# Node numbers and the weighing's exponentials in one PSUM bank for VectorE; each exponential taken twice

## The chip, the cores and the metric
One core of a Trainium2 chip. The metric is the time of one launch in microseconds (us) on the device, as the median of several runs. Engines: PE is TensorE (PEld its weight load), DVE is VectorE, ACT is ScalarE, POOL is GpSimd, and SP only issues transfers.

## What is computed
The network takes 6250 node rows of 256 numbers and 200000 edges sorted by destination. `x` is normalised, a graph transformer of two attention layers and a linear attention ("mix") over all nodes are added to it, and then a mixture of experts with a graph router. The change lies in the two attention layers:

```python
def gt_layer(edge_index, embeds, qT, kT, vT, ln_s, ln_b):      # D = 128, HEAD = 8 heads of 16
    rows, cols = (edge_index[0], edge_index[1])
    q = (embeds[rows] @ qT).reshape(-1, HEAD, hd)
    k = (embeds[cols] @ kT).reshape(-1, HEAD, hd)
    v = (embeds[cols] @ vT).reshape(-1, HEAD, hd)
    att = jnp.clip(jnp.einsum('ehd,ehd->eh', q, k), -10.0, 10.0)
    expAtt = jnp.exp(att)
    attNorm = jax.ops.segment_sum(expAtt, rows, num_segments=n)[rows]
    att = expAtt / (attNorm + 1e-08)
    res = (att[..., None] * v).reshape(-1, d)
    agg = jax.ops.segment_sum(res, rows, num_segments=n)
    # then: add embeds, layer norm
```

## The kernel before
The kernel sorts the edges by the tile of 125 nodes that their `rows` end lies in (50 tiles), so that each tile of 128 edges belongs to one node tile. `attend` then works through 1668 edge tiles in 417 groups of four (GROUP = 4). It is called twice, as att1 (with `Keys` beside it, which prepares the linear attention) and att2 (with `Mix` beside it, which finishes it). Nothing else uses the changed lines.

A group passes these stations. GpSimd issues four indirect gathers (L700), each of 128 rows of 256 numbers (keys and values) from HBM to `kv_e`, a ring of four groups (SLOTS = 4). SP loads the node numbers of the edges as rows (`local`, L681). VectorE compares them with a pointer scalar `lane_no` into `hot_t` (near_hot, L811, one SBUF tensor of 512 bf16 values). TensorE multiplies `hot_t` with the node tile's queries into PSUM `ps_q` (fetch_q, L761). VectorE forms the products of `ps_q` with the keys (dots, L798), sums them by head (sum_dots, L817) and clips the sums (clip, L830). ScalarE takes the exponential into the last 8 columns of `vals` (exps, L784). VectorE multiplies the values with these exponentials (weigh, L822: both inputs in SBUF, the exponentials repeated 16 times). It also builds the one-hot matrix `hot` by comparing `node_no`, 500 node numbers held in SBUF, with the edges' own (one_hot, L804: both inputs in SBUF). TensorE adds up `hot` times `vals` into PSUM `ps_sum` (add_up, L773), and VectorE adds that to `acc` (add_sums, L838, twice per group).

The order on each engine is written out by hand: `edge_steps` unrolls all steps, and in step n each part handles group n plus its lag. VectorE's list is

```python
            edge_steps(dve, total, [(0, dots), (2, near_hot), (0, sum_dots), (-1, weigh), (0, clip), (1, one_hot),
                                    (-2, add_sums)], lambda n: side.vector(dve, n), side.last)
```

so that it weighs group n-1 between the head sums and the clip of group n. `side` is `Keys` or `Mix`, whose instructions stand behind each step's on each engine; a node tile of theirs is spread over steps 8 apart. A gather of group k waits until group k-4 has been weighed (`used=m["weighted"]` in `gather_rows`). `vals`, `clipped`, `hot_t`, `ps_q` and `ps_sum` are double buffers; `prod` is single. In att2 all eight PSUM banks are held: two `ps_q`, two `ps_sum` and Mix's `ps_t`, `ps_q`, `ps_o`, `ps_h`.

Of the kernel before, what the change touches and what calls it, by code (L numbers as in the profile page):

```python
# [7 lines left out]
ALU = mybir.AluOpType  # L8
# [8 lines left out]
LANES = 128  # L17
# [692 lines left out]
def attend(nc, c, name, g, qs, kv, acc, beside):  # L710

    with ExitStack() as st:
# [3 lines left out]
        def psum(n):  # L716
# [9 lines left out]
        vals = sb("vals", [LANES, 2, GROUP, SUMS])  # L726
        tile_of = sb("tile_of", [1, g.pairs], I32)
        ps_q, ps_sum = psum("ps_q"), psum("ps_sum")
        m = sem_set(nc, st, name, ["tiles_in", "one_hots", "near_hots", "q_ready", "prods",
                                   "dots", "clips", "exps", "weighted", "summed", "added"])  # L730
        m["gathered"] = c.gathered[name]
        m["local_in"] = st.enter_context(semaphores(nc, [f"{name}_local_in{j}" for j in range(SLOTS)]))
        total = g.edge_tiles // GROUP
# [15 lines left out]
        @block.tensor  # L749
        def _(pe):  # L750
            pe.wait_ge(m["tiles_in"], 16)
            numbers = TileNumbers(nc, pe, tile_of, g)

            def fetch_q(k, r, j):

                pe.wait_ge(m["near_hots"], k + 1)
                wait(pe, m["prods"], k - 1)
                for p in range(per):
                    t = numbers.of(k * per + p)
                    for e in range(PAIR * p, PAIR * (p + 1)):  # L760
                        ins = pe.matmul(ps_q[j % 2][:, e * D:(e + 1) * D], hot_t[:, j % 2, e * LANES:(e + 1) * LANES],  # L761
                                        at(qs, t), start=True, stop=True)
                ins.then_inc(m["q_ready"], 1)
                numbers.load((k + 1) * per)

            def add_up(k, r, j):

                pe.wait_ge(m["weighted"], k + 1)
                pe.wait_ge(m["one_hots"], k + 1)
                wait(pe, m["added"], 2 * (k - 2) + 2)  # L770
                for p in range(GROUP // PAIR):
                    for e in range(PAIR):
                        ins = pe.matmul(ps_sum[j % 2][0:NODE_TILE, p * 256:p * 256 + SUMS],  # L773
                                        hot[:, j, PAIR * p + e, :], vals[:, j % 2, PAIR * p + e, :],
                                        start=e == 0, stop=e == PAIR - 1)
                ins.then_inc(m["summed"], 1)
            edge_steps(pe, total, [(-2, add_up), (1, fetch_q)], lambda n: side.tensor(pe, n), side.last)

        @block.scalar
        def _(act):  # L780
            def exps(k, r, j):
                act.wait_ge(m["clips"], k + 1)
                wait(act, m["summed"], k - 1)
                act.activation(vals[:, j % 2, :, D:SUMS],  # L784
                               clipped[:, j % 2, :].rearrange("p (e h) -> p e h", e=GROUP), ACT.Exp)\
                    .then_inc(m["exps"], 1)
            edge_steps(act, total, [(0, exps)], lambda n: side.scalar(act, n), side.last)

        @block.vector
        def _(dve):  # L790
            dve.wait_ge(m["tiles_in"], 16)
            numbers = TileNumbers(nc, dve, tile_of, g)

            def dots(k, r, j):
                dve.wait_ge(m["q_ready"], k + 1)
                dve.wait_ge(m["gathered"][j], (r + 1) * (16 * GROUP))
                wait(dve, m["dots"], k)
                dve.tensor_tensor(prod[:].rearrange("p (e d) -> p e d", e=GROUP),  # L798
                                  ps_q[j % 2][:, :].rearrange("p (e d) -> p e d", e=GROUP),
                                  kv_e[:, j, :, 0:D], ALU.mult).then_inc(m["prods"], 1)  # L800

            def one_hot(k, r, j):
                wait(dve, m["summed"], (k - SLOTS) + 1)
                dve.tensor_tensor(hot[:, j], c.node_no[:],  # L804
                                  own_tile(g, k), ALU.is_equal)\
                    .then_inc(m["one_hots"], 1)

            def near_hot(k, r, j):
                dve.wait_ge(m["local_in"][j], (r + 1) * 16)
                wait(dve, m["q_ready"], k - 1)  # L810
                dve.tensor_scalar(hot_t[:, j % 2, :], local[0:NODE_TILE, j], c.lane_no[0:NODE_TILE, :], None, ALU.is_equal)\  # L811
                    .then_inc(m["near_hots"], 1)

            def sum_dots(k, r, j):
                dve.wait_ge(m["prods"], k + 1)
                wait(dve, m["clips"], k - 1)
                dve.tensor_reduce(dots_sb[:, j % 2, :], prod[:].rearrange("p (h d) -> p h d", d=HEAD),  # L817
                                  AX, ALU.add).then_inc(m["dots"], 1)

            def weigh(k, r, j):  # L820
                dve.wait_ge(m["exps"], k + 1)
                dve.tensor_tensor(vals[:, j % 2, :, 0:D].rearrange("p e (h d) -> p e h d", d=HEAD),  # L822
                                  kv_e[:, j, :, D:2 * D].rearrange("p e (h d) -> p e h d", d=HEAD),
                                  vals[:, j % 2, :, D:SUMS].unsqueeze(3).broadcast_to([LANES, GROUP, HEADS, HEAD]),
                                  ALU.mult).then_inc(m["weighted"], 1)

            def clip(k, r, j):
                dve.wait_ge(m["dots"], k + 1)
                wait(dve, m["exps"], k - 1)
                dve.tensor_scalar(clipped[:, j % 2, :], dots_sb[:, j % 2, :], -10.0, 10.0, ALU.max, ALU.min)\  # L830
                    .then_inc(m["clips"], 1)

            def add_sums(k, r, j):
                dve.wait_ge(m["summed"], k + 1)
                for p in range(per):
                    a = at(acc, numbers.of(k * per + p))
                    wait(dve, m["added"], 2 * k + p)
                    dve.tensor_tensor(a, a, ps_sum[j % 2][0:NODE_TILE, p * 256:p * 256 + SUMS], ALU.add)\  # L838
                        .then_inc(m["added"], 1)
                numbers.load((k + 1) * per)  # L840
            edge_steps(dve, total, [(0, dots), (2, near_hot), (0, sum_dots), (-1, weigh), (0, clip), (1, one_hot),
                                    (-2, add_sums)], lambda n: side.vector(dve, n), side.last)


# [137 lines left out]
class Mix:  # L982

    def __init__(self, nc, c, ins, st, X, mean, rstd, mean_rstd, mix_rstd, key_values, key_sums):
# [16 lines left out]
        self.square, self.scaled = self.xr, sb("scaled", [NODE_TILE, GIN])  # L1001
        self.shift = sb("shift", [NODE_TILE, GIN])
        self.ms = sb("ms", [NODE_TILE, self.tiles])
        self.ps_t, self.ps_q, self.ps_o, self.ps_h = (psum(n) for n in ("ps_t", "ps_q", "ps_o", "ps_h"))
        self.m = sem_set(nc, st, "mix", ["w_in", "w_ready", "normed", "turned", "turned_sb", "q_ps", "q_copied",
                                         "q_min", "q_exped", "q_ready", "o_ps", "den", "inverse", "o_ready", "h_ps",
                                         "h_base", "h_out", "squared", "stepped", "shifted", "ms", "root", "roots", "scaled",
# [117 lines left out]
    def tensor(self, pe, n):  # L1125
        m, two = self.m, self.two
        t = self.tile_at(n, 3)
        if t is not None:
            pe.wait_ge(m["normed"], t + 1)
            wait(pe, m["turned_sb"], t)  # L1130
            for ch in range(KC):
                turn = pe.transpose(self.ps_t[:, ch * NODE_TILE:(ch + 1) * NODE_TILE],
                                    self.xr[:, ch * LANES:(ch + 1) * LANES], self.c.ident[0:NODE_TILE, 0:NODE_TILE])
# [1311 lines left out]
```

## Time and profile before

| | us |
|---|---|
| runs, median of 3 (lowest, highest) | 7925.82 (7924.39, 7932.85) |
| the profiled execution, its own time | 7930.16 |
| its span | 7927.9 |
| att1 (1218 to 3410 of the span) | 2192 |
| att2 (3515 to 5706) | 2191 |
| busy over the span: PE, DVE, ACT, POOL | 5293.5, 5852.9, 1022.4, 5163.2 |

Busy shares are averages over stages with different limits. What is worth reading for this change are the two attention stages. An engine's busy time counts its own instructions; the time from one gather's end to the next one's start is not in it.

### The profile page before, as it was taken

What the parts mean: (1) busy time and instruction counts of PE and PEld (TensorE: products, weight loads), DVE (VectorE), ACT (ScalarE), POOL (GpSimd) and SP (SyncE); (2) the same over time, 40 slices, a digit from 0 to 9 for tenths busy, and PEclk for the clock granted to TensorE, in tenths of its full rate; (3) what the DMA queues carried; (4) which work ended last, traced back from release to release, by engine and by line L of the source; (5) the groups of instructions that cost most, each with busy time, mean ns of one, the idle gap of its engine ahead of it and who ended that gap; (6) DMA issues with size and microseconds to landing.
All of it is one profiled execution on the core that took longest, in us unless ns stands there. A gap on an engine that the chain in (4) does not pass through costs nothing. (4 is left out here: it accounts for less than half of the span.)

```text
span 7927.9 us, 103405 instructions
## 1 busy us (share of the span) xinstructions
PE 5293.5 (67%) x27325; PEld 4204.5 (53%) x27325; DVE 5852.9 (74%) x15897; ACT 1022.4 (13%) x3273; POOL 5163.2 (65%) x5420
## 2 busy tenths in 40 slices
PE   5886855665665566556666666666559999999441
PEld 3553534555555555535555555555546666666331
DVE  7878845666666666667787878877766777777997
ACT  0000010000000000020000000000132222222230
POOL 2331306777777777737777777777617777777892
PEclk7555578778778877877887778878758888888555
DMA  1000034444444444434444444444432333332336
GB/s 31 3 3 8 3 95 125 129 128 129 128 129 128 128 129 130 128 97 126 126 127 126 125 125 126 126 125 126 125 82 52 63 62 57 62 63 55 114 96 179
DMA packets 504010, 776.97 MB, mean 98 GB/s; under 512 B 121545, under 2 KB 364222, under 8 KB 503442
## 3 DMA queue, kind: packets, MB, share of 16 engines
q0 software_dynamic: 202656, 454.22, 21.7%
q1 hardware_dynamic: 292838, 304.95, 14.7%
q10 hardware_dynamic: 7948, 11.21, 0.6%
q8 instruction: 237, 3.88, 0.2%
q14 instruction: 331, 2.71, 0.1%
HBM read 698.60 MB, written 71.36 MB: 97 GB/s over the span
## 5 line engine op out<-in xcount | busy, mean ns | idle before, releaser
L700 POOL DMA_INDIRECT att_kv_e<-kv,gnn_idx x3336 | 3366.1, 1009 | 1196.5 <-issue 1004.8
L773 PE MATMUL att_ps_sum<-att_vals,att_hot 128*125 128x136 f32 x6672 | 1345.1, 361 | 1638.6 <-DVE att_vals L822 1637.8
L773 PEld LDWEIGHTS att_ps_sum<-att_vals,att_hot 128*125 128x125 f32 x6672 | 1131.4, 246 | 1852.8 <-DVE att_vals L822 1845.7
L700 POOL DMA_INDIRECT max_rows<-rows,gat_idx x1128 | 1064.8, 944 | 568.3 <-issue 329.0
L798 DVE TENSOR_TENSOR att_prod<-att_ps_q,att_kv_e 128x512 f32<-128x512 f32 x834 | 575.9, 690 | 999.6 <-DMA att_kv_e<-kv,gnn_idx 633.5
L761 PE MATMUL att_ps_q<-qs,att_hot_t 125*128 x6672 | 1217.8, 344 | 26.9 <-DVE att_hot_t L811 26.9
L761 PEld LDWEIGHTS att_ps_q<-qs,att_hot_t 125*128 125x128 f32 x6672 | 1167.1, 262 | 28.1 <-issue 28.1
L1854 DVE CUSTOM_DVE_ANT_0 max_junk<-max_far,max_ps_b 125x256 bf16<-125x256 bf16 x2256 | 792.5, 416 | 259.2 <-PE max_ps_b L1818 256.1
L784 ACT ACTIVATE att_vals<-att_clipped 128x32 f32<-128x32 f32 x834 | 191.3, 229 | 4049.9 <-DVE att_clipped L830 4049.9
L838 DVE TENSOR_TENSOR acc<-acc,att_ps_sum 125x136 f32 x1668 | 484.4, 290 | 123.1 <-PE att_ps_sum L773 2.8
L822 DVE TENSOR_TENSOR att_vals<-att_kv_e,att_vals 128x512 f32<-128x512 f32 x834 | 567.6, 681 | 0.0
L817 DVE TENSOR_REDUCE att_dots<-att_prod 128x32 f32<-128x512 f32 x834 | 564.6, 677 | 0.1
L804 DVE TENSOR_TENSOR att_hot<-node_no,gnn_loc 128x500 f32<-128x500 f32 x834 | 558.4, 670 | 0.0
L2253 PE MATMUL ex_ps_o<-ex_w,ex_hid 128*125 128x256 f32 x1600 | 518.6, 480 | 0.0
L811 DVE TENSOR_SCALAR att_hot_t<-att_local,lane_no 125x512 f32<-125x512 bf16 x834 | 406.4, 487 | 42.3 <-DMA att_local<-gnn_loc_rows 42.3
L509 POOL DMA_INDIRECT gnn_table<-gnn_records,gnn_dest_sb x120 | 174.3, 1452 | 401.7 <-DVE gnn_records L425 372.2
L1818 PE MATMUL max_ps_b<-max_a_t,pick_head 12*125 12x512 bf16 x1128 | 375.6, 434 | 64.5 <-ACT max_a_t L1827 51.8
L2264 PE MATMUL ex_ps_h<-ex_xT,ex_w 128*128 128x250 f32 x1600 | 413.5, 404 | 0.0
L2253 PEld LDWEIGHTS ex_ps_o<-ex_w,ex_hid 128*125 128x125 f32 x1600 | 356.0, 234 | 89.4 <-issue 14.0
L480 PE MATMUL gnn_ps_perm<-gnn_moves,gnn_hot_low 125*128 125x96 f16 x1600 | 327.9, 387 | 81.6 <-DVE gnn_moves L430 81.6
L2264 PEld LDWEIGHTS ex_ps_h<-ex_xT,ex_w 128*128 128x128 f32 x1600 | 342.7, 214 | 57.9 <-issue 0.4
L480 PEld LDWEIGHTS gnn_ps_perm<-gnn_moves,gnn_hot_low 125*128 125x128 f16 x1600 | 235.2, 150 | 188.5 <-DVE gnn_moves L430 113.1
(445 smaller groups left out, 6887.5 us busy)
## 6 DMA issues: line engine op xcount, KB each, us to landing
att_local<-gnn_loc_rows SPq DMA_DIRECT2D x834, 128.0 KB
att_kv_e<-kv,gnn_idx POOLq DMA_INDIRECT x3336, 3.0
max_local<-gat_loc_rows SPq DMA_DIRECT2D x282, 128.0 KB
gs_local<-gat_loc_rows SPq DMA_DIRECT2D x141, 256.0 KB, 3.3
outs<-ex_y SPq DMA_DIRECT2D x25, 896.0 KB
max_rows<-rows,gat_idx POOLq DMA_INDIRECT x1128
ans_late<-outs SPq DMA_DIRECT2D x11, 896.0 KB
ans_early<-outs SPq DMA_DIRECT2D x8, 896.0 KB
```

The lines of the kernel that those rows point to most:

```text
L480: ins = pe.matmul(ps_perm[k % 2][:, 0:2 * SLOTS_F], hot_low[:, k % 2, :, w], moves[:, k % 2, :, :, w], start=w == 0, stop=w == BLOCK - 1)
L700: pool.indirect_dma_start(rows(j, e), None, source, bass.IndirectOffsetOnAxis(ap=g.idx[:, t:t + 1], axis=0))\
L761: ins = pe.matmul(ps_q[j % 2][:, e * D:(e + 1) * D], hot_t[:, j % 2, e * LANES:(e + 1) * LANES], at(qs, t), start=True, stop=True)
L773: ins = pe.matmul(ps_sum[j % 2][0:NODE_TILE, p * 256:p * 256 + SUMS], hot[:, j, PAIR * p + e, :], vals[:, j % 2, PAIR * p + e, :], start=e ...
L798: dve.tensor_tensor(prod[:].rearrange("p (e d) -> p e d", e=GROUP), ps_q[j % 2][:, :].rearrange("p (e d) -> p e d", e=GROUP), kv_e[:, j, : ...
L804: dve.tensor_tensor(hot[:, j], c.node_no[:], own_tile(g, k), ALU.is_equal)\
L817: dve.tensor_reduce(dots_sb[:, j % 2, :], prod[:].rearrange("p (h d) -> p h d", d=HEAD), AX, ALU.add).then_inc(m["dots"], 1)
L822: dve.tensor_tensor(vals[:, j % 2, :, 0:D].rearrange("p e (h d) -> p e h d", d=HEAD), kv_e[:, j, :, D:2 * D].rearrange("p e (h d) -> p e h ...
L838: dve.tensor_tensor(a, a, ps_sum[j % 2][0:NODE_TILE, p * 256:p * 256 + SUMS], ALU.add)\
L1854: ins = dve.tensor_tensor_reduce(out=junk[:, j % 2, 2 * n + i, :], in0=far[:, j % 2, i * 256:(i + 1) * 256], in1=ps_b[n][0:NODE_TILE, i * ...
L2253: ins = pe.matmul(self.ps_o[0:NODE_TILE, 0:GIN], self.hid[:, e % 2, hc, k * NODE_TILE:(k + 1) * NODE_TILE], self.w2[:, e, hc, :], start=hc ...
L2264: ins = pe.matmul(self.ps_h[:, i * TWO:(i + 1) * TWO].rearrange("p (t n) -> p t n", t=2), self.w1[:, e, ch, a:a + LANES], self.xT[:, s % 2 ...
```

## The change
The node numbers (125 of them, in place of 4 x 125) are copied once per attention by VectorE into a PSUM bank of their own, `ps_dve`, and `one_hot` reads them there, repeated over the group. ScalarE takes each exponential twice: first into the same bank (`weights`, one buffer), where `weigh` reads it, then into `vals`, where TensorE needs it. New semaphores keep the two apart: `exps` for the PSUM copy, `exps_out` for the one in `vals`. `weigh` now itself waits for the sums of two groups back, and TensorE's `add_up` waits for `exps_out`. `one_hot` moves ahead of `clip` in VectorE's list. To free a bank, Mix's turned tile and its queries share one, and the turning waits until the last queries were copied.

```diff
+        ps_dve = st.enter_context(nc.psum_tensor(f"{name}_ps_dve", [LANES, 512], F32))
+        node_no = ps_dve[:, 0:NODE_TILE]
+        weights = ps_dve[:, LANES:LANES + GROUP * HEADS].rearrange("p (e h) -> p e h", e=GROUP)
...
             def add_up(k, r, j):
                 pe.wait_ge(m["weighted"], k + 1)
+                pe.wait_ge(m["exps_out"], k + 1)
...
             def exps(k, r, j):
                 act.wait_ge(m["clips"], k + 1)
+                scores = clipped[:, j % 2, :].rearrange("p (e h) -> p e h", e=GROUP)
+                act.activation(weights, scores, ACT.Exp).then_inc(m["exps"], 1)
                 wait(act, m["summed"], k - 1)
-                act.activation(vals[:, j % 2, :, D:SUMS],
-                               clipped[:, j % 2, :].rearrange("p (e h) -> p e h", e=GROUP), ACT.Exp)\
-                    .then_inc(m["exps"], 1)
+                act.activation(vals[:, j % 2, :, D:SUMS], scores, ACT.Exp).then_inc(m["exps_out"], 1)
...
             def one_hot(k, r, j):
+                if k == 0:
+                    dve.tensor_copy(node_no, c.node_no[:, 0, :]).then_inc(m["node_nos"], 1)
+                    dve.wait_ge(m["node_nos"], 1)
                 wait(dve, m["summed"], (k - SLOTS) + 1)
-                dve.tensor_tensor(hot[:, j], c.node_no[:],
-                                  own_tile(g, k), ALU.is_equal)\
+                dve.tensor_tensor(hot[:, j], over(node_no, GROUP), own_tile(g, k), ALU.is_equal)\
                     .then_inc(m["one_hots"], 1)
...
             def weigh(k, r, j):
                 dve.wait_ge(m["exps"], k + 1)
+                wait(dve, m["summed"], k - 1)
                 dve.tensor_tensor(vals[:, j % 2, :, 0:D].rearrange("p e (h d) -> p e h d", d=HEAD),
                                   kv_e[:, j, :, D:2 * D].rearrange("p e (h d) -> p e h d", d=HEAD),
-                                  vals[:, j % 2, :, D:SUMS].unsqueeze(3).broadcast_to([LANES, GROUP, HEADS, HEAD]),
+                                  weights.unsqueeze(3).broadcast_to([LANES, GROUP, HEADS, HEAD]),
                                   ALU.mult).then_inc(m["weighted"], 1)
             def clip(k, r, j):
                 dve.wait_ge(m["dots"], k + 1)
-                wait(dve, m["exps"], k - 1)
+                wait(dve, m["exps_out"], k - 1)
...
-            edge_steps(dve, total, [(0, dots), (2, near_hot), (0, sum_dots), (-1, weigh), (0, clip), (1, one_hot),
+            edge_steps(dve, total, [(0, dots), (2, near_hot), (0, sum_dots), (-1, weigh), (1, one_hot), (0, clip),
...
-        self.ps_t, self.ps_q, self.ps_o, self.ps_h = (psum(n) for n in ("ps_t", "ps_q", "ps_o", "ps_h"))
+        turned_q, self.ps_o, self.ps_h = (psum(n) for n in ("ps_t_q", "ps_o", "ps_h"))
+        self.ps_t, self.ps_q = turned_q[:, 0:self.two], turned_q[:, self.two:2 * self.two]
...
             wait(pe, m["turned_sb"], t)
+            wait(pe, m["q_copied"], t)
```

## Rows read from the trace of the kernel before

**Rows 1.** Windows over both attentions: stretch, length, busy time by engine, clock, DMA.
```profile
1218.00:3410.00 2192.00, 1328.43 (x7056) 1180.31 (x7056) 1474.37 (x3432) 148.65 (x567) 1682.79 (x1668) 0.79 0.46 129
3515.00:5706.00 2191.00, 1401.73 (x7850) 1271.47 (x7851) 1728.19 (x3980) 190.66 (x647) 1683.02 (x1668) 0.80 0.45 126
```

**Rows 2.** Costliest lines: count, busy us, mean ns, idle before and what ended it.
```profile
L700 POOL DMA_INDIRECT att_kv_e<-kv,gnn_idx x3336 | 3366.1, 1009 | 1196.5 <-issue 1004.8 <-POOLq L85 180.8 <-DVE att_vals L822 11.0
...
L798 DVE TENSOR_TENSOR att_prod<-att_ps_q,att_kv_e 128x512 f32<-128x512 f32 x834 | 575.9, 690 | 999.6 <-DMA att_kv_e<-kv,gnn_idx 633.5 <-issue 215.3 <-PE att_ps_q L761 147.6
L822 DVE TENSOR_TENSOR att_vals<-att_kv_e,att_vals 128x512 f32<-128x512 f32 x834 | 567.6, 681 | 0.0
...
L804 DVE TENSOR_TENSOR att_hot<-node_no,gnn_loc 128x500 f32<-128x500 f32 x834 | 558.4, 670 | 0.0
...
L784 ACT ACTIVATE att_vals<-att_clipped 128x32 f32<-128x32 f32 x834 | 191.3, 229 | 4049.9 <-DVE att_clipped L830 4049.9
```

**Rows 3.** Waits, att1: total us, times, longest.
```profile
POOL att_kv_e L700 <- DVE att_vals L822: 9.1, 30, 0.3
```

**Rows 4.** Tile kv_e, the gathers: ns min/median/max, first and last start.
```profile
L700 POOL DMA_INDIRECT att_kv_e<-kv,gnn_idx x3336: 942/946/1570, 1218.6 to 5705.0; - x197
```

**Rows 5.** Timeline (start, us): first and last gather stretched in one_hot or weigh.
```profile
1228.25 0.67 DVE L804 TENSOR_TENSOR att_hot<-node_no,gnn_loc 128x500 f32<-128x500 f32 x1
...
1228.73 1.01 POOL L700 DMA_INDIRECT att_kv_e<-kv,gnn_idx  x1 [0.30 <-issue]
...
5704.84 0.68 DVE L822 TENSOR_TENSOR att_vals<-att_kv_e,att_vals 128x512 f32<-128x512 f32 x1
5704.99 1.35 POOL L700 DMA_INDIRECT att_kv_e<-kv,gnn_idx  x1 [0.30 <-issue]
```

**Rows 6.** Timeline: first and last gather stretched in near_hot (L811).
```profile
1284.53 0.48 DVE L811 TENSOR_SCALAR att_hot_t<-att_local,lane_no 125x512 f32<-125x512 bf16 x1
1284.68 1.14 POOL L700 DMA_INDIRECT att_kv_e<-kv,gnn_idx  x1 [0.30 <-issue]
...
5699.64 0.48 DVE L811 TENSOR_SCALAR att_hot_t<-att_local,lane_no 125x512 f32<-125x512 bf16 x1
5699.92 1.02 POOL L700 DMA_INDIRECT att_kv_e<-kv,gnn_idx  x1 [0.30 <-issue]
```

**Rows 7.** Timeline: gathers beside the products, a later weighing, the adds.
```profile
2005.44 0.69 DVE L798 TENSOR_TENSOR att_prod<-att_ps_q,att_kv_e 128x512 f32<-128x512 f32 x1 [0.95 <-DMA att_kv_e<-kv,gnn_idx]
2005.54 0.95 POOL L700 DMA_INDIRECT att_kv_e<-kv,gnn_idx  x1 [0.30 <-issue]
...
2006.79 0.95 POOL L700 DMA_INDIRECT att_kv_e<-kv,gnn_idx  x1 [0.30 <-issue]
2007.24 0.68 DVE L822 TENSOR_TENSOR att_vals<-att_kv_e,att_vals 128x512 f32<-128x512 f32 x1
...
2050.16 0.73 DVE L838 TENSOR_TENSOR acc<-acc,att_ps_sum 125x136 f32 x2
2050.69 0.95 POOL L700 DMA_INDIRECT att_kv_e<-kv,gnn_idx  x1 [0.30 <-issue]
```

**Rows 8.** Timeline: a gather late in near_hot, and one behind Keys' scaling.
```profile
1234.92 0.47 DVE L917 TENSOR_SCALAR keys_wkv<-keys_wkv,keys_w 128x512 f32<-128x512 f32 x1
1235.05 1.16 POOL L700 DMA_INDIRECT att_kv_e<-kv,gnn_idx  x1 [0.30 <-issue]
...
3401.48 0.48 DVE L811 TENSOR_SCALAR att_hot_t<-att_local,lane_no 125x512 f32<-125x512 bf16 x1
3401.83 0.95 POOL L700 DMA_INDIRECT att_kv_e<-kv,gnn_idx  x1 [0.30 <-issue]
```

**Rows 9.** Timeline: the weighing and the gather reusing its rows, at their closest.
```profile
3531.34 0.68 DVE L822 TENSOR_TENSOR att_vals<-att_kv_e,att_vals 128x512 f32<-128x512 f32 x1
...
3535.64 1.42 POOL L700 DMA_INDIRECT att_kv_e<-kv,gnn_idx  x1 [0.30 <-DVE att_vals L822]
```

More of the change, by code:

```diff
@@ L728, in attend @@
         ps_q, ps_sum = psum("ps_q"), psum("ps_sum")
-        m = sem_set(nc, st, name, ["tiles_in", "one_hots", "near_hots", "q_ready", "prods",
-                                   "dots", "clips", "exps", "weighted", "summed", "added"])
+        ps_dve = st.enter_context(nc.psum_tensor(f"{name}_ps_dve", [LANES, 512], F32))
+        node_no = ps_dve[:, 0:NODE_TILE]
+        weights = ps_dve[:, LANES:LANES + GROUP * HEADS].rearrange("p (e h) -> p e h", e=GROUP)
+        m = sem_set(nc, st, name, ["tiles_in", "node_nos", "one_hots", "near_hots", "q_ready", "prods",
+                                   "dots", "clips", "exps", "exps_out", "weighted", "summed", "added"])
         m["gathered"] = c.gathered[name]
```

## Prediction

> **What bounds the kernel now.** I read the profile's page first, for the stage in which the changed code runs and for its costliest lines. The windows then gave each stage's busy time, the waits showed who waits for whom, and the timeline showed single instructions beside each other. The changed code runs only in the two attentions, 2192 and 2191 us of the span, with 1668 gathers in each [rows 1]. In both, GpSimd issues one gather after another. It is busy for 1682.8 and 1683.0 us [rows 1]. Of the 1196.5 us that it sits idle before gathers, 180.8 come before the two attentions begin and 1004.8 are "issue", 0.3 us for each of the 3336 [rows 2]. The rest is called a wait for the weighing, but no such wait is over 0.3 us, the ordinary gap [rows 3]. So nothing holds the gathers back: 1668 of them at 1009 ns [rows 2], with (2191 - 1683) / 1667 = 305 ns between them, are the whole stage. VectorE is busy for 1474 and 1728 us of it [rows 1] and waits 633.5 us for gathered rows [rows 2]. TensorE, ScalarE and the DMA engines (0.46 busy) are further off [rows 1]. A faster gather is the only thing that shortens these stages. Time saved elsewhere is worth nothing.
>
> How fast can a gather be? The fastest takes 942 ns, the median 946, the slowest 1570 [rows 4]. The mean of 1009 is above the median: a minority is stretched, by 3366.1 - 3336 x 0.947 = 207 us in all (0.947 is the mean of the gathers that start with none of the instructions named below beside them; three are in [rows 7]). What stretches them is the question that decides this forecast.
>
> **Who stretches the gathers.** I laid each of the 3336 gathers beside the VectorE instruction that was under way when it started.
> - The weighing and the one-hot compare read two SBUF tensors. 625 stretched gathers (over 0.97 us) start inside one of them or within 0.05 us of its start; the first and the last are [rows 5]. A one-hot compare alone, 0.19 us from its end, cost 0.06 us. A weighing just begun, with the compare behind it, cost 0.40 us. Summed over the 625: 146 us, of which 18 fall on 87 gathers that start inside the compare itself and 117 on those that start inside the weighing.
> - The transposed one-hot (L811) is a compare with one SBUF tensor and a pointer scalar. 387 stretched gathers of the 502 that start inside it; first and last are [rows 6]. Sum: 60 us. It would be easy to put this to the weighing, which follows about a microsecond later while the gather still runs. This speaks against it. The stretch grows with how much of L811 is left when the gather starts (0.20 us left: 1.02; 0.33 us left: 1.14 [rows 6]). With 0.13 us left the gather takes 0.95, though the weighing follows it as it follows the others [rows 8]. And a weighing that begins 0.45 us into a gather leaves it at 0.95 [rows 7]. The Keys scaling (L917), again one SBUF tensor with a pointer scalar, makes a gather 1.16 us with neither weighing nor one-hot compare near [rows 8].
> - The products (L798) read one operand from PSUM. A gather that starts 0.10 us into them takes 0.95 [rows 7]; so does one that starts within the adds of the sums, which read PSUM too [rows 7].
> So a gather is sensitive close behind its start, to instructions that take two SBUF tensors or that are of the compare-with-scalar kind, and not to those with a PSUM operand.
>
> The Trainium skill, "GPSIMD Engine Reference", Specifications, names just these two kinds as contending with GpSimd: two SBUF inputs, or a 2-port perf mode. By that rule, the trace agrees. The Trainium skill, "SBUF — State Buffer", section "SBUF: two separate sides", makes it a lock held for the whole instruction; the trace does not bear that out (a weighing that began 0.45 us into a gather kept its 0.68 us, and the gather its 0.95). By the rule as it stands L811 would stay a blocker after the change, which is what the rows say too.
>
> **The change part by part.**
> 1. The one-hot compare takes its node numbers, and the weighing its exponentials, from PSUM. Both then have one SBUF and one PSUM operand, like the products and the adds. What it removes is the 146 us above, if the form alone decides. In VectorE time it costs what the products differ by: 690 ns against 681 and 670 [rows 2, 7], so at most 20 ns per instruction, 834 x 2 x 20 ns = 33 us over both stages, beside 463 us and more that VectorE idles in each stage [rows 1]. On the path: nothing.
> 2. The L811 stretch stays. Its place relative to the gathers is set by when the fourth gather's rows land, counted from that gather's end, and the three gathers behind it are not among those that the weighing stretches. So the number of collisions should be as before: 60 us stay. The bounds are 0 and 834 x 0.22 us = 183 us (each compare hitting at its worst).
> 3. The one-hot compare moves ahead of the clip. The clip is a short instruction with one SBUF tensor (0.17 us). It now comes 0.6 us later, followed by the adds. A gather starting in its last 0.1 us could lose that much; with one in eight doing so, 834 / 8 x 0.05 = 5 us. I take 3, bounds 0 and 40 (half of them at 0.1).
> 4. ScalarE's second exponential: 834 x 229 ns = 191 us [rows 2] on an engine busy for 149 and 191 us of 2190 [rows 1]. Hidden by that idle time. TensorE's sums wait for it; it ends some 0.5 us behind the clip, a whole group before they need it. Its wait for the sums is for those of two groups back. Mix's and Keys' ScalarE work queued behind it starts 0.2 us later in steps 5 us long.
> 5. The weighing's own new wait (sums of two groups back), one exponential buffer in place of two, and the clip behind the compare: all make VectorE later by tenths. The cover is the slack between a weighing's end and the gather that reuses its rows. The smallest in both attentions is 3.62 us, from 3531.34 + 0.68 to 3535.64 [rows 9]. Four groups shortened by some 0.18 us each take 0.7 us of it. If it were gone, each microsecond would stand on the path.
> 6. One tensor_copy per attention, and Mix's turned tile and queries in one bank with a wait for a copy made five steps earlier: nothing.
>
> Sum: 146 - 3 = 143 us. Against the profiled execution's 7930.2 us (span 7927.9 and 2.3 around it) that makes 7787; the median of the runs is 4.3 us lower, so **7783 us**.
>
> **Rivals.**
> - *All of the stretch goes.* The L811 class was mine to separate; were its stretch in truth the weighing's, 207 us go: 7719. For it: a weighing does follow in nearly every one. Against it: the gather at 0.95 and the Keys scaling [rows 8].
> - *Only one of the two edits frees the port*, say because a PSUM operand in second place (the weighing) or a repeated one (the node numbers) counts differently. Part of the weighing's 117 us is the compare's behind it (a start early in the weighing outlasts it). Estimated from the 117 and 18: only the compare freed, some 35 us, 7891; only the weighing freed, some 110 us, 7816. Against it: the products have PSUM first, the adds second, and neither stretches [rows 7].
> - *L811 or the clip gives it back.* If the shorter group moved the compares so that twice as many collide, 60 more stay: 7843. It decides only if landing times from the gather's end change; DMA load rises from 0.46 to about 0.48.
> - *Nothing changes.* Only the compare-with-scalar kind stretches gathers, and two SBUF inputs never do. L811 and the clip, which stay, would then be behind all 207 us, and the time would be 7926. Against it stands the gather at 1.01 that starts inside a one-hot compare with 0.19 us of it left [rows 5]. The Trainium skill, "SBUF — State Buffer", in the box on SWDGE in "SBUF: two separate sides", names only the 2-port mode as what keeps GpSimd from writing descriptors, and counts two SBUF inputs only against a GpSimd instruction that reads SBUF.
> - *Slower: VectorE becomes the bound.* Place: the clip, exponential, weighing loop in the second attention, where Mix runs beside it and only (2191 - 1728) / 417 = 1.1 us per group is idle. Were PSUM operands or the new waits to add over 1.1 us per group, the gathers would wait for the weighing; at 1.5 us more, 417 x 0.4 = 167 us on that stage, so 7926 + 167 - 73 saved in the first = 8020. Against it: a PSUM form adds 20 ns, not hundreds.
>
> **How the numbers follow.** Forecast 0.76 (own range 7766 to 7802: the clip's and L811's bounds taken at a fifth); all gone 0.07; one edit only 0.06; given back 0.05; nothing 0.03; slower 0.03. 0.2% is 16 us, about what a measurement of this kernel can tell from no change: faster 0.94, same 0.03, slower 0.03. The range must leave out at most 0.2: 7756 to 7830 takes in the forecast's range with room for half a give-back and for the weighing-only case.
>
> **What would show it.** After the change the gather's mean should be 0.966 us (1009 - 143 us / 3336), its median still 946, and each attention about 72 us shorter. Stretched gathers should all start inside L811's compare, at most 1.2 us long; none should start inside the weighing or the one-hot compare. These two should take 680 to 700 ns. GpSimd should still wait for nothing but issue. A mean near 0.947 means that L811 was innocent, one over 0.98 that one of the two forms still blocks or that more compares collide. VectorE waits in GpSimd's list would show the slower case.

## The result and the profile after

The changed kernel takes 7745.4 us (median; 7742.9 to 7747.0), against 7925.1 before: ratio 0.9772, 95% interval 0.9755 to 0.9788. That is 180 us less. The forecast was 7783 us, 143 less, and its range ended at 7756: the direction and the way of the gain were right, one term of the sum was not.

The windows over both attentions, as in [rows 1] (stretch, length, busy time and instructions of PE, PEld, DVE, ACT, POOL, clock, DMA share, GB/s). Each stretch runs from the first gather to the last one's landing:

```profile
1214.00:3310.00 2096.00, 1312.64 (x7048) 1167.91 (x7048) 1472.73 (x3429) 197.79 (x981) 1587.16 (x1667) 0.78 0.48 134
3415.00:5520.00 2105.00, 1373.29 (x7856) 1245.59 (x7856) 1724.67 (x3983) 240.79 (x1063) 1595.57 (x1668) 0.81 0.47 131
```

The costliest lines, which answer to [rows 2]:

```profile
L700 POOL DMA_INDIRECT att_kv_e<-kv,gnn_idx x3336 | 3184.0, 954 | 1192.4 <-issue 970.4 <-POOLq L85 176.3 <-DVE att_vals L829 45.7
...
L829 DVE TENSOR_TENSOR att_vals<-att_kv_e,att_ps_dve 128x512 f32<-128x512 f32 x834 | 563.1, 675 | 0.0
L811 DVE TENSOR_TENSOR att_hot<-att_ps_dve,gnn_loc 128x500 f32<-128x500 f32 x834 | 557.7, 669 | 0.1
...
L817 DVE TENSOR_SCALAR att_hot_t<-att_local,lane_no 125x512 f32<-125x512 bf16 x834 | 417.0, 500 | 42.5 <-DMA att_local<-gnn_loc_rows 42.5
L790 ACT ACTIVATE att_vals<-att_clipped 128x32 f32<-128x32 f32 x834 | 177.5, 213 | 0.0
L788 ACT ACTIVATE att_ps_dve<-att_clipped 128x32 f32<-128x32 f32 x834 | 167.7, 201 | 3770.5 <-DVE att_clipped L837 3770.5
```

The tile view of the gathers (ns min/median/max), against [rows 4], and their waits for the weighing from 1300 to 3300 us, in the first attention, against [rows 3]:

```profile
L700 POOL DMA_INDIRECT att_kv_e<-kv,gnn_idx x3336: 942/947/1212, 1215.1 to 5519.0; - x197
```
```profile
POOL att_kv_e L700 <- DVE att_vals L829: 23.2, 76, 0.3
```

The gathers fell from 3366.1 to 3184.0 us, mean 1009 to 954 ns. These 182 us are the whole change of the span (185 us; the first gather starts 3.5 us sooner). Their median did not move and the slowest went from 1570 to 1212 ns: the tail is gone, not the body. Inside the two attentions GpSimd still waits for nothing longer than its ordinary 0.3 us. VectorE's two new forms are no slower than the old ones (675 and 669 ns; before 681 and 670), and ScalarE's second exponential adds 154 us (345.2 for both, 191.3 before) on an engine that is idle for nine tenths.

In this kernel near_hot is L817, the one-hot compare L811, the weighing L829, the products L802. The timeline (start, duration) of a gather that starts 0.14 us into the weighing, and of one 0.16 us into near_hot:

```profile
3103.68 0.68 DVE L829 TENSOR_TENSOR att_vals<-att_kv_e,att_ps_dve 128x512 f32<-128x512 f32 x1
3103.82 0.95 POOL L700 DMA_INDIRECT att_kv_e<-kv,gnn_idx  x1 [0.30 <-issue]
...
4131.10 0.48 DVE L817 TENSOR_SCALAR att_hot_t<-att_local,lane_no 125x512 f32<-125x512 bf16 x1
4131.26 1.14 POOL L700 DMA_INDIRECT att_kv_e<-kv,gnn_idx  x1 [0.30 <-issue]
```

The first took 1.35 us before [rows 5] and takes 0.95 now. The second is as long as in [rows 6]. Both edits did what they were to do, and L811 of the kernel before (I call it near_hot from here on, since its line number moves) stretches as it did. What changed is how often it hits. Each gather again laid beside the VectorE instruction under way when it starts:

| stretch of the gathers that start inside, us (number stretched) | before | after |
|---|---|---|
| weighing, one-hot compare, and within 0.05 us of their start | 146 (625) | 0 |
| near_hot | 60 (387) | 12 (89) |
| products (near_hot starts 0.36 to 0.49 us into the gather) | 1 (14) | 4 (62) |
| Mix's and Keys' instructions (most with two SBUF tensors or a pointer scalar) | 2 | 9 |

Summed, some 207 us of stretch became 25. The third row is a second way in which near_hot holds a gather, which the prediction did not have: it starts when the gather has run for 0.36 to 0.49 us, and the gather takes up to 1.06 us. Started a little later, 0.48 to 0.78 us into a gather, near_hot is itself held: it takes up to 0.72 us in place of 0.48 and ends 1.2 us behind the gather's start (34 times before, 145 after). That costs nothing here, since VectorE has room. Both in the changed kernel:

```profile
1243.34 1.05 POOL L700 DMA_INDIRECT att_kv_e<-kv,gnn_idx  x1 [0.30 <-issue]
1243.80 0.47 DVE L817 TENSOR_SCALAR att_hot_t<-att_local,lane_no 125x512 f32<-125x512 bf16 x1
...
1475.26 0.95 POOL L700 DMA_INDIRECT att_kv_e<-kv,gnn_idx  x1 [0.30 <-issue]
1475.77 0.68 DVE L817 TENSOR_SCALAR att_hot_t<-att_local,lane_no 125x512 f32<-125x512 bf16 x1
```

The weighing does neither: one that starts 0.45 us into a gather leaves it at 0.95 and takes its own 0.68 [rows 7], and so do all that start 0.36 to 0.78 us into one in the trace of experiment 2.

### The profile page after: what moved, and what is told of

Its sections match the earlier page's. It is cut to its first block and busy times, and to the rows that moved or that the text cites. A ratio compares the mean times of both kernels' runs of the same rounds, so it can differ in the third digit from the quotient of the medians.

```text
span 7742.7 us, 105071 instructions
## 1 busy us (share of the span) xinstructions
PE 5244.2 (68%) x27325; PEld 4162.3 (54%) x27325; DVE 5849.7 (76%) x15899; ACT 1122.4 (14%) x4107; POOL 4983.5 (64%) x5420
## 5 line engine op out<-in xcount | busy, mean ns | idle before, releaser
L700 POOL DMA_INDIRECT att_kv_e<-kv,gnn_idx x3336 | 3184.0, 954 | 1192.4 <-issue 970.4
L777 PE MATMUL att_ps_sum<-att_vals,att_hot 128*125 128x136 f32 x6672 | 1309.9, 354 | 1500.5 <-DVE att_vals L829 1499.8
L777 PEld LDWEIGHTS att_ps_sum<-att_vals,att_hot 128*125 128x125 f32 x6672 | 1103.2, 240 | 1711.2 <-DVE att_vals L829 1701.7
L802 DVE TENSOR_TENSOR att_prod<-att_ps_q,att_kv_e 128x512 f32<-128x512 f32 x834 | 573.7, 688 | 817.1 <-DMA att_kv_e<-kv,gnn_idx 531.6
L788 ACT ACTIVATE att_ps_dve<-att_clipped 128x32 f32<-128x32 f32 x834 | 167.7, 201 | 3770.5 <-DVE att_clipped L837 3770.5
L829 DVE TENSOR_TENSOR att_vals<-att_kv_e,att_ps_dve 128x512 f32<-128x512 f32 x834 | 563.1, 675 | 0.0
L811 DVE TENSOR_TENSOR att_hot<-att_ps_dve,gnn_loc 128x500 f32<-128x500 f32 x834 | 557.7, 669 | 0.1
L817 DVE TENSOR_SCALAR att_hot_t<-att_local,lane_no 125x512 f32<-125x512 bf16 x834 | 417.0, 500 | 42.5 <-DMA att_local<-gnn_loc_rows 42.5
```

The costliest lines, as they stand in the source:

```text
L700: pool.indirect_dma_start(rows(j, e), None, source, bass.IndirectOffsetOnAxis(ap=g.idx[:, t:t + 1], axis=0))\
L811: dve.tensor_tensor(hot[:, j], over(node_no, GROUP), own_tile(g, k), ALU.is_equal)\
```

## Experiments

There were ten runs, the last two of them repeats. The means below are those of the gathers, in the profiled execution. Chips differ: on the four that were used the kernel before took 7925.1 (the result above), 7927.9 (experiments 1 to 4), 7939.5 (5 to 7) and 7935.1 us (8 to 10). So a time goes by its ratio to the kernel before on its own chip, and differences of some 10 us between chips mean nothing.

**1. near_hot off the port too.** To the changed kernel one edit:

```diff
+                if k == 0: dve.tensor_copy(lane_ps, c.lane_no[:])          # lane_ps: one column of the PSUM bank
+                wait(dve, m["exps"], k - 2)
-                dve.tensor_scalar(hot_t[:, j % 2, :], local[0:NODE_TILE, j], c.lane_no[0:NODE_TILE, :], None, ALU.is_equal)
+                dve.tensor_tensor(hot_t[:, j % 2, :], local[0:NODE_TILE, j], lane_ps[0:NODE_TILE].broadcast_to(...), ALU.is_equal)
```

> The changed kernel with one more instruction moved off two SBUF ports: L811's compare takes the lane number from the PSUM bank (tensor_tensor, one SBUF and one PSUM operand) in place of a pointer scalar. Theory A (a gather is stretched by what VectorE runs when the gather starts, and L811 is of the stretching kind): the gathers that start inside L811's compare in the changed kernel carry 12 us of stretch and those just before it 4 us; these 16 us go, the gather's mean falls from 954 to about 949 ns, time 7729, and what stays is Mix's and Keys' instructions. L811 grows from 500 to about 670 ns beside idle time. Theory B (L811 was never to blame, the weighing was): mean stays 954, time 7745 or a little more.

Measured: 7725.9 us (ratio to before 0.9743, 0.9726 to 0.9759), mean 949 ns, as theory A had it. The line and a gather 0.16 us into the longer compare:

```profile
L821 DVE TENSOR_TENSOR att_hot_t<-att_local,att_ps_dve 125x512 f32<-125x512 bf16 x834 | 564.3, 677 | 12.5 <-DMA att_local<-gnn_loc_rows 12.4
```
```profile
3524.69 0.68 DVE L821 TENSOR_TENSOR att_hot_t<-att_local,att_ps_dve 125x512 f32<-125x512 bf16 x1
3524.85 0.95 POOL L700 DMA_INDIRECT att_kv_e<-kv,gnn_idx  x1 [0.31 <-issue]
```

The compare itself went from 500 to 677 ns, and the kernel became faster (on one chip in experiments 9 and 10). No gather that starts inside near_hot is stretched any more, and 9 us of stretch are left in all, on Mix's and Keys' instructions.

**2. The same edit on the kernel before**, where weighing and one-hot compare still read two SBUF tensors.

> The kernel before with L811's compare alone taken off (lane number from PSUM); weighing and one-hot compare still read two SBUF tensors. Theory A: the 60 us of stretch of the gathers that start inside L811 go, the gather's mean falls from 1009 to about 991 ns, time about 7865; if the longer compare (670 in place of 487 ns) pushes the weighing onto other places of a gather, between 7840 and 7900. Theory B (L811 innocent): 7925, and the gathers that start inside L811 are as long as before.

Measured: 7941.0 us (ratio 1.0018, 1.0009 to 1.0028), mean 1015 ns. Both theories missed. Theory A's first half holds: 485 gathers start 0.03 to 0.43 us behind a near_hot's start, none over 0.96. Its sum does not: the stretch inside weighing and compare grew from 146 to some 225 us. A gather beside each (timeline; near_hot L816, weighing L828):

```profile
2936.75 0.68 DVE L816 TENSOR_TENSOR att_hot_t<-att_local,att_ps_dve 125x512 f32<-125x512 bf16 x1
2936.88 0.94 POOL L700 DMA_INDIRECT att_kv_e<-kv,gnn_idx  x1 [0.30 <-issue]
...
2895.18 0.68 DVE L828 TENSOR_TENSOR att_vals<-att_kv_e,att_vals 128x512 f32<-128x512 f32 x1
2895.34 1.34 POOL L700 DMA_INDIRECT att_kv_e<-kv,gnn_idx  x1 [0.30 <-issue]
```

The share of each instruction was read rightly, but the shares don't subtract: taking one hold away moves where the next gathers start, and 583 in place of 312 now start inside the weighing. The gather behind one that near_hot met started mostly 0.61 us behind the weighing's start (median; 0.98 us long) and now starts 0.24 us behind it (1.26 us long). A part of this shift is the longer compare, which puts the weighing 0.2 us later behind near_hot; without that the gather would start some 0.44 us in, an estimate, and in this trace the gathers there take 1.11 us. The two were not run apart. The same edit gains 20 to 25 us on the changed kernel and loses 13 here, by what else holds the gathers.

**3 and 4. One operand at a time.** From the changed kernel, either the node numbers or the exponentials (then taken once) back in SBUF; the order stays the new one.

```diff
 3: -  dve.tensor_tensor(hot[:, j], over(node_no, GROUP), own_tile(g, k), ALU.is_equal)
    +  dve.tensor_tensor(hot[:, j], c.node_no[:], own_tile(g, k), ALU.is_equal)
 4: -  act.activation(weights, scores, ACT.Exp).then_inc(m["exps"], 1)
    -  ... weights.unsqueeze(3) ...
    +  ... vals[:, j % 2, :, D:SUMS].unsqueeze(3) ...
```

> The changed kernel with the node numbers back in SBUF: the weighing alone is freed, the one-hot compare (in its new place ahead of the clip) reads two SBUF tensors. Theory A: the compare stretches gathers that start inside it, the weighing none; of the 207 us of stretch some 110 to 150 go, time 7780 to 7816. Theory C (the PSUM operand of the weighing, in second place and repeated 16 times, does not free the port): 7890 or more, with stretched gathers inside the weighing.

> The changed kernel with the weighing's exponentials back in SBUF, each taken once: the one-hot compare alone is freed. Theory A: gathers that start inside the weighing are stretched, those in the one-hot compare are not; some 35 to 90 us of 207 go, time 7835 to 7890. Theory D (the repeated PSUM operand of the compare does not free the port): about 7925, with stretched gathers inside the compare.

Measured: 7800.8 us with the weighing alone freed (0.9837, 0.9820 to 0.9853), 7863.2 with the compare alone freed (0.9918, 0.9901 to 0.9934); means 976 and 989 ns. Both as theory A. (The order of compare and clip is the new one in both, so they are not the shares of the kernel before.) Timeline of the first (weighing L826 from PSUM, compare L808 from SBUF), then of the second (weighing L827 from SBUF, compare L810 from PSUM):

```profile
3268.20 0.68 DVE L826 TENSOR_TENSOR att_vals<-att_kv_e,att_ps_dve 128x512 f32<-128x512 f32 x1
3268.34 0.95 POOL L700 DMA_INDIRECT att_kv_e<-kv,gnn_idx  x1 [0.30 <-issue]
...
3284.76 0.67 DVE L808 TENSOR_TENSOR att_hot<-node_no,gnn_loc 128x500 f32<-128x500 f32 x1
3284.96 1.28 POOL L700 DMA_INDIRECT att_kv_e<-kv,gnn_idx  x1 [0.30 <-DVE att_vals L826]
```
```profile
3100.59 0.68 DVE L827 TENSOR_TENSOR att_vals<-att_kv_e,att_vals 128x512 f32<-128x512 f32 x1
3100.75 1.34 POOL L700 DMA_INDIRECT att_kv_e<-kv,gnn_idx  x1 [0.30 <-issue]
...
4427.73 0.67 DVE L810 TENSOR_TENSOR att_hot<-att_ps_dve,gnn_loc 128x500 f32<-128x500 f32 x1
4427.87 0.95 POOL L700 DMA_INDIRECT att_kv_e<-kv,gnn_idx  x1 [0.30 <-DVE att_vals L827]
```

A PSUM operand frees the gather whether it stands first or second, repeated along the outer or the inner dimension. In both kernels near_hot's stretch lies between the 60 us of before and the 12 of after: 19 and 37 us.

**5. Why near_hot hits less often.** near_hot stands 0.6 us behind the products, and these start when a group's fourth gather has landed. From the end of that gather to the products' start it is 2.18 us (median, first attention) before and 2.47 after. The distance decides whether near_hot hits. The gathers behind the fourth start 0.31, 1.56 and 2.81 us behind its end. With 2.1 us near_hot starts at 2.7, 0.1 us before the third of these, which it then holds; with 2.47 it starts at 3.1 and has missed it. Before, 468 of the 834 groups had a distance of 1.87 to 2.17 us and carried 57 of near_hot's 60 us; after, 63 groups have it.

What moves the distance? Before, in 721 groups the third or the fourth gather was stretched (over 0.02 us), and there the median is 2.06 to 2.11 us; in the 112 with neither it is 2.60. After, 671 groups have neither, with 2.48. Experiments 2, 3, 4, 7 and 8 show the same sign (fourth gather stretched by over 0.15 us: 1.94 to 2.13; neither stretched: 2.47 to 2.69). Experiment 6 below does not: 2.89 and 2.85. My reading is that gathers that are held up give the transfers ahead of them time to clear. The largest of these is `att_local`, 128 KB per group, issued just behind near_hot. So in the changed kernel I loaded it for the first four groups only:

```diff
         wait(sp, used, (k - SLOTS) + 1)
         sp.nop(nofuse=True)
+        if k >= SLOTS: return
...
-                dve.wait_ge(m["local_in"][j], (r + 1) * 16)
+                dve.wait_ge(m["local_in"][j], 16)
```

> The changed kernel with the edges' node numbers loaded for the first four groups only, and used again for all others (so the queries fetched are wrong ones; the instructions are the same). It tells why the products start 2.45 us behind the end of a group's fourth gather in the changed kernel, and 2.06 to 2.14 us behind it where that gather was stretched. Theory E (the rows queue in the DMA engines behind the 128 KB of node numbers and behind the gathers before): without these loads the products start 2.0 to 2.2 us behind the fourth gather, L811 comes to lie on the start of the gather again, and the gather's mean rises from 954 towards 965 ns, time 7760 to 7785, although there is less to do. Theory F (the landing has nothing to do with the loads): 2.45 us and 7745 stay.

Measured: 7757.4 us (0.9765, 0.9749 to 0.9781), mean 958 ns. By its ratio it is as fast as the changed kernel (0.9772 and 0.9775), with a fifth less data to move; its gathers take 3197.0 us in all, against 3184.0 and 3188.2 in the two traces of the changed kernel. The products start 1.89 us behind the fourth gather (median), whether the third and fourth were stretched or not. 706 gathers now start 0.05 to 0.45 us behind near_hot's start in place of 158, but mostly at its far end, where it costs little: 30 us. The windows show the DMA share down from 0.48, and the timeline a typical group (products L804, near_hot L819):

```profile
1214.00:3320.00 2106.00, 1312.56 (x7056) 1165.83 (x7056) 1469.49 (x3433) 198.11 (x983) 1596.73 (x1668) 0.79 0.38 108
```
```profile
2402.60 0.94 POOL L702 DMA_INDIRECT att_kv_e<-kv,gnn_idx  x1 [0.30 <-issue]
2402.92 0.69 DVE L804 TENSOR_TENSOR att_prod<-att_ps_q,att_kv_e 128x512 f32<-128x512 f32 x1 [1.41 <-DMA att_kv_e<-kv,gnn_idx]
2403.53 0.48 DVE L819 TENSOR_SCALAR att_hot_t<-att_local,lane_no 125x512 f32<-125x512 bf16 x1
2403.85 0.98 POOL L702 DMA_INDIRECT att_kv_e<-kv,gnn_idx  x1 [0.30 <-issue]
```

Theory E holds in kind, by the distance and by near_hot's stretch: the loads set when the rows land, and that sets where near_hot falls. The time alone does not tell the theories apart. It came out a little under the expected range, since 1.89 lies below the 2.0 that I had taken, and near_hot then hits late, where a hit is short. That the loads delay the rows is shown; that a held gather shortens the distance by letting these transfers clear is argued, and which rows wait behind which stays open.

**6. near_hot elsewhere.** If only its place counts, moving it must cost what its new place predicts:

```diff
-  [(0, dots), (2, near_hot), (0, sum_dots), (-1, weigh), ...
+  [(0, dots), (0, sum_dots), (2, near_hot), (-1, weigh), ...
```

> The changed kernel with L811's compare moved behind the head sums, 0.6 us later in the step; the same instructions. Theory A (a gather is stretched when L811 is under way at its start): L811 then starts 0.08 to 0.34 us ahead of a gather for products that start 2.52 to 2.78 us behind the fourth gather, a third of the groups, against 99 of 834 groups now; its stretch rises from 12 to 30 to 50 us, time 7760 to 7785. Rival (where L811 lies does not matter): 7745.

Measured: 7772.8 us (0.9786, 0.9770 to 0.9803), mean 962 ns, some 35 us of stretch inside near_hot in place of 12, which is theory A. A gather of it, 0.17 us into near_hot: 

```profile
3671.32 0.48 DVE L817 TENSOR_SCALAR att_hot_t<-att_local,lane_no 125x512 f32<-125x512 bf16 x1
3671.49 1.13 POOL L700 DMA_INDIRECT att_kv_e<-kv,gnn_idx  x1 [0.30 <-issue]
```

The same instructions in another order make the gathers 21 to 25 us longer (3208.9 us against 3184.0 and 3188.2), on an engine that in the changed kernel is idle for 18 to 30% of the stages. The ratio is 0.0011 to 0.0014 above those of the changed kernel, inside their intervals, so the time alone does not show it. Nor did only near_hot's place move: `att_local` is issued behind it, and the products now start 2.73 us behind the fourth gather, not 2.47.

**7. The order by itself.** On the kernel before:

```diff
-  (-1, weigh), (0, clip), (1, one_hot),
+  (-1, weigh), (1, one_hot), (0, clip),
```

> The kernel before with the one-hot compare moved ahead of the clip, nothing else. In the prediction this part had a price of its own only through the clip: theory A says that the compare starts 0.08 us sooner, all forms stay of the stretching kind, the stretch stays near 207 us, time 7910 to 7940, and the products start as long behind the fourth gather as before (2.1 us). Rival: the order is what moved the products' start to 2.45 us, and a part of the 180 us is the order's; time under 7900.

Measured: 8057.0 us (1.0146, 1.0129 to 1.0163), mean 1058 ns. Both were wrong: it costs some 120 us. The trace says where; it is of the slowest of the five executions, 8095.8 us, and so shows more than the median, 166 us over the profiled one of before. The two attentions are 2274 and 2280 us long:

```profile
1216.00:3490.00 2274.00, 1383.68 (x7056) 1231.48 (x7056) 1474.36 (x3435) 148.43 (x567) 1761.89 (x1668) 0.75 0.45 124
3590.00:5870.00 2280.00, 1451.12 (x7856) 1318.38 (x7856) 1728.66 (x3984) 191.27 (x647) 1768.26 (x1668) 0.77 0.44 121
```

About 405 gathers, in the kernel before as here, start almost exactly 0.60 us behind a weighing's start. The gather ahead of nine in ten of them was held by near_hot (389 of 408 before, 358 of 403 here), and so ends at a fixed distance from what VectorE does next. Timeline (near_hot L811, weighing L822, compare L804):

```profile
2868.39 0.48 DVE L811 TENSOR_SCALAR att_hot_t<-att_local,lane_no 125x512 f32<-125x512 bf16 x1
2868.64 1.04 POOL L700 DMA_INDIRECT att_kv_e<-kv,gnn_idx  x1 [0.31 <-issue]
...
2869.38 0.68 DVE L822 TENSOR_TENSOR att_vals<-att_kv_e,att_vals 128x512 f32<-128x512 f32 x1
2869.97 0.67 DVE L804 TENSOR_TENSOR att_hot<-node_no,gnn_loc 128x500 f32<-128x500 f32 x1
2869.99 1.48 POOL L700 DMA_INDIRECT att_kv_e<-kv,gnn_idx  x1 [0.30 <-issue]
```

With the clip between, the compare starts 0.13 us later, and the gather that starts at the same distance gets away. From the trace of the kernel before:

```profile
3676.09 1.07 POOL L700 DMA_INDIRECT att_kv_e<-kv,gnn_idx  x1 [0.30 <-issue]
...
3676.87 0.68 DVE L822 TENSOR_TENSOR att_vals<-att_kv_e,att_vals 128x512 f32<-128x512 f32 x1
...
3677.47 0.95 POOL L700 DMA_INDIRECT att_kv_e<-kv,gnn_idx  x1 [0.30 <-issue]
3677.60 0.67 DVE L804 TENSOR_TENSOR att_hot<-node_no,gnn_loc 128x500 f32<-128x500 f32 x1
```

Those gathers take 1.39 us in the mean here and 0.99 before: 403 x 0.39 = 157 us, about the growth of the stretch from 207 to 371. If that is the cause, another short instruction in the clip's old place must win it back.

**8. A useless instruction added.** To kernel 7, ahead of the compare:

```diff
+                    dve.tensor_scalar(junk[:], dots_sb[:, (k - 1) % 2, :], -10.0, 10.0, ALU.max, ALU.min)
```

> The kernel of the order alone (compare ahead of the clip, all in SBUF, 8057 us) with one more short instruction between the weighing and the compare, a clip of the same 128x32 numbers into a scratch tile that nothing reads. Theory G: 411 gathers start 0.60 us behind a weighing's start, because the gather before was held by L811 and ended at a fixed distance from it; there the compare, when it follows the weighing at once, is just under way and holds them (1.39 us), and when the clip stands between (kernel before) it starts a little later than the gather's sensitive point (0.99 us). With the filler the compare is back at its old place: those gathers fall to about 1.0, the stretch from 368 to 200 to 230 us, and one more instruction makes the kernel faster, 7915 to 7955. Rival (the later clip and exponential, or the length of the step, cost the 130 us): 8057 or more.

Measured: 7937.2 us (1.0002, 0.9992 to 1.0011), mean 1011 ns, stretch 215 us; 429 gathers start 0.60 us behind a weighing and take 1.015 in the mean. Theory G. The timeline (filler L807, compare L810):

```profile
3568.31 0.68 DVE L828 TENSOR_TENSOR att_vals<-att_kv_e,att_vals 128x512 f32<-128x512 f32 x1
3568.91 0.22 DVE L807 TENSOR_SCALAR att_junk<-att_dots 128x32 f32<-128x32 f32 x1
3568.91 0.95 POOL L700 DMA_INDIRECT att_kv_e<-kv,gnn_idx  x1 [0.30 <-issue]
3569.04 0.67 DVE L810 TENSOR_TENSOR att_hot<-node_no,gnn_loc 128x500 f32<-128x500 f32 x1
```

Some 830 instructions whose result nothing reads made that kernel about 115 us faster (ratio 1.0146 to 1.0002). In experiment 4, where the compare reads PSUM and the order is the new one, 272 gathers start at the same 0.60 us and take 0.95: the PSUM operand makes the place harmless too.

**9 and 10. The changed kernel and the better one on one chip.**

> The changed kernel itself, on the same chip as the next one: 7745, gather mean 954 ns.

> The changed kernel with L811's lane number from PSUM, against the changed kernel on the same chip: theory A has the 16 us of stretch around L811 gone, 7726 to 7730; the rival, that the two differ by chance between chips, has both within 5 us of each other.

Measured: 7755.4 us (7752.8 to 7757.5; ratio to before 0.9775, 0.9762 to 0.9789) and 7730.9 (7730.0 to 7733.6; 0.9745, 0.9732 to 0.9758), means 956 and 950 ns. On this chip the version of experiment 1 is 24.5 us under the changed kernel (20 between the two chips of before), and its runs and those of the changed kernel do not overlap. It beats both kernels.

Not tried: the PSUM operands with the old order. So what the new order is worth with both of them stays open.

## The prediction, step by step

- *The gather is the bound, nothing but its length matters.* Right: 182 of the 185 us of span are the gathers' own, and in all twelve traces the span less the gathers' time is 4550 to 4563 us.
- *Part 1, the two PSUM operands remove 146 us and cost nothing.* Right: no gather inside weighing or compare is stretched after, and experiments 3 and 4 show it for each operand alone. The new forms did not take the 20 ns more.
- *Part 2, "L811's stretch stays ... the number of collisions should be as before: 60 us stay."* This step failed, and it is the term that put the forecast 37 us too high. 16 us stayed (12 inside near_hot, 4 ahead of it), 44 less than priced; Mix's and Keys' instructions, which had no term, took 7 us more than before. Its argument was that the landing, counted from the fourth gather's end, would not move. It moved from 2.18 to 2.47 us, past the place at which near_hot hits: of 468 groups at 1.87 to 2.17 us 63 are left. Shown is that the distance goes with whether the third or fourth gather was stretched (2.06 to 2.11 against 2.60 us in the trace of before already, which the prediction did not use), and that without `att_local` it falls to 1.89 us (experiment 5). Why it does so, by transfers that have more time to clear, is argued. The sentence that the three gathers behind the fourth are not stretched by the weighing looks at the wrong gathers: those ahead of the landing decide. That L811 and not the weighing was behind the 60 us was right (experiments 1, 2 and 6).
- *Part 3, the clip costs 3 us.* 0.6 us, and at its other end: 159 gathers start inside it, and only those in its first 0.03 us are longer, by some 0.02 us; in its last 0.1 us all take 0.95. (In experiment 6, where 218 gathers start at that first place, it is 5 us.) But the order of compare and clip was priced for the PSUM form alone. In the SBUF form it costs 120 us (experiments 7 and 8). The change needs the compare's PSUM operand to bear its own order.
- *Parts 4 to 6, nothing on the path.* Right: both exponentials together 345 us, and in the attentions GpSimd never waits over 0.3 us.
- *Rivals.* "All of the stretch goes" (7719) and the forecast (7783) were the ends between which the time fell, and for neither's reason. "One edit only" is refuted by experiments 3 and 4; its estimates of 7816 and 7891 stand against 7801 and 7863. "Gives it back" named the right condition, landing times that change, and had the wrong sign. "Nothing changes" and "slower" did not occur: an instruction with two SBUF inputs does stretch gathers (experiments 3 and 4).
- *What would show it.* The mean of 954 ns lay between the 966 of the forecast and the 947 of the rival; stretched gathers start inside near_hot, or, 62 of them, inside the products just ahead of it, or inside Mix's and Keys' instructions, and these two I had not named.

The two rules of the Trainium skill come out so. The Trainium skill, "GPSIMD Engine Reference", Specifications, names two SBUF inputs or a 2-port mode as contending with GpSimd: by that rule, the trace agrees for the weighing and the compare, each with its operand in SBUF (1.35 and 1.28 us) and in PSUM (0.95). near_hot holds gathers with a pointer scalar (1.14) and not with a PSUM operand (0.95); that it runs in a 2-port mode no run shows. The Trainium skill, "SBUF — State Buffer", section "SBUF: two separate sides", has the pair locked for the whole instruction by whoever starts first. The runs agree in part. A gather that near_hot holds is let go with near_hot's end (it is 0.05 us shorter for each 0.05 us that near_hot started earlier). But a gather in progress did not hold a weighing that started 0.45 us behind it [rows 7], and it held a near_hot only when that started 0.48 to 0.78 us behind it.

## What to carry to other kernels

Where GpSimd's gathers are the bound, list what VectorE runs when each gather starts, and move one operand of what stretches them to PSUM, even if the instruction gets longer or an engine with room has to write the operand twice. Do not subtract such shares one from another: each hold that goes moves all later starts, and a hold's price is a matter of 0.1 us in place. So try the set, not the parts, and expect that a reordering that looks free costs or gives a per cent.

## What I had not expected of the hardware

- The stretch depends on the place to within 0.05 us and repeats. For near_hot, by how long before the gather it started: 0.35 us: 0.95; 0.30: 1.00; 0.25: 1.04; 0.20: 1.09; 0.15: 1.15; 0.10: 1.20; 0.05 and 0: 0.95. All nine traces in which near_hot has its pointer scalar give the same medians, to 0.01 us.
- There is a second place, and it works both ways: near_hot started 0.36 to 0.49 us into a gather stretches it, and started 0.48 to 0.78 us into it is stretched itself, to end 1.2 us behind the gather's start. The weighing shows neither.
- Holds synchronise the engines: 408 gathers of 3336 start within 0.02 us of 0.60 us behind a weighing's start in the kernel before, 403 in experiment 7 and 429 in 8. Without near_hot's hold 18 do (experiment 1) and 8 (experiment 2).
- A fifth fewer bytes to move made the gathers 9 to 13 us longer and the kernel no faster (experiment 5), a useless instruction made one faster by some 115 (experiment 8), and a compare 177 ns longer made one faster by 20 to 25 (experiments 1 and 10).
